# Cross-attention and quantised feed-forward on one core: accumulating copies, half-wise waits of the first key product, and a reordered VectorE queue

## The reference

```
x   = x + attention(layernorm(x), ctx, ctx, mask)     # 16 heads of 64, softmax over 361
out = x + ffn(layernorm(x))                           # 256 -> 1024, gelu, 1024 -> 256
```

## Time and profile before

| | us |
|---|---|
| median of 3 runs | 1116.12 (1115.36 to 1117.17) |
| the profiled execution, its own time | 1116.15 |
| its span, first to last instruction | 1114.3 |
| mean granted TensorE clock | 0.992 |
| PE busy | 1026.3 (92%) |
| DVE busy | 982.0 (88%) |
| ACT busy | 866.6 (78%) |
| POOL busy | 770.5 (69%) |

### The profile page before, as it was taken

How to read it: one execution, slowest core, us unless ns; L and a number is a source line. 1 busy time by engine, 2 the same in 40 slices (tenths; PEclk the granted TensorE clock), 3 DMA queues, 4 the chain that set the end, 5 groups by cost and what they waited for, 6 DMA issues and landing times.

```text
span 1114.3 us, 37739 instructions
## 1 busy us (share of the span) xinstructions
PE 1026.3 (92%) x10639; PEld 649.0 (58%) x10639; DVE 982.0 (88%) x2538; ACT 866.6 (78%) x1809; POOL 770.5 (69%) x1106
## 2 busy tenths in 40 slices
PE   4999999999999999999999999999999999998828
PEld 2555566666666666666666666666666666665317
DVE  5776999999999999999999999999999999996997
ACT  4555888888888888888888888888888888886906
POOL 2337777777777777777777777777777777774800
PEclk9999999999999999999999999999999999999969
DMA  8301665555555555555555555555555555554003
GB/s 260 109 1 29 130 131 136 136 132 132 131 129 135 136 136 136 134 129 133 136 133 129 134 132 129 135 136 129 128 135 136 135 131 129 132 136 143 1 0 119
DMA packets 435437, 136.77 MB, mean 123 GB/s; under 512 B 407666, under 2 KB 434390, under 8 KB 435414
## 3 DMA queue, kind: packets, MB, share of 16 engines
q1 hardware_dynamic: 435414, 136.47, 51.0%
HBM read 28.60 MB, written 6.55 MB: 32 GB/s over the span
## 4 chain that ended last, share of the span: by engine, by line
PE 75%; DVE 10%; ACT 6%; issue 4%; POOL 3%; DVEq 1%; DMA 1%; ACTq 1%; SPq 0%; POOLq 0%
PE front L366 19%; PE front L368 17%; PE front L367 17%; PE back L1300 8%; PE front L1278 6%; PE tp L1278 5%; POOL hl L610 3%; DVE hrange L1129 2%; DVE hrange L1130 2%; DVE prob L979 2%; ACT prob L736 2%; DVE k_l L1028 1%; ACT q_h L790 1%; ACT ctx_h L786 1%; PE front L1415 1%
## 5 line engine op out<-in xcount | busy, mean ns | idle before, releaser
L610 POOL TENSOR_TENSOR hl<-prob,hl 100x361 f16<-100x361 f32 x511 | 432.0, 855 | 96.6 <-DVE hl L986 50.7
L736 ACT ACTIVATE prob<-prob,nmax 100x361 f32<-100x361 f32 x512 | 293.8, 586 | 47.7 <-DVE nmax L979 47.6
L366 PE MATMUL front<-ctx_h,wk_h 128*128 128x362 f16 x512 | 164.2, 321 | 31.6 <-POOL ctx_l L599 18.0
L1300 PEld LDWEIGHTS back<-v,pT 128*128 128x128 f16 (+1 forms) x4608 | 163.9, 97 | 38.9 <-issue 9.6
L742 ACT ACTIVATE hl<-prob 100x361 f16<-100x361 f32 x352 | 176.1, 500 | 7.9
L1300 PE MATMUL back<-v,pT 128*128 128x65 f16 (+1 forms) x4608 | 172.8, 193 | 0.6 <-DMA pT<-hl 0.5
L368 PE MATMUL front<-ctx_h,wk_l 128*128 128x362 f16 x512 | 161.7, 316 | 0.0
L367 PE MATMUL front<-ctx_l,wk_h 128*128 128x362 f16 x512 | 161.5, 315 | 0.0
L746 ACT ACTIVATE k_h<-front 128x362 f16<-128x362 f32 x256 | 119.0, 465 | 54.6 <-PE front L368 54.6
L1028 DVE SCALAR_TENSOR_TENSOR k_l<-front,k_h 128x362 f16<-128x362 f32 x256 | 135.2, 528 | 24.3 <-ACT k_h L746 21.6
L979 DVE CUSTOM_DVE_ANT_0 prob<-front,mask_g,ngain 100x361 f32<-100x361 f32 x256 | 149.6, 585 | 2.3
(11 more groups left out here) (205 smaller groups left out, 2006.5 us busy)
## 6 DMA issues: line engine op xcount, KB each, us to landing
ctx_raw<-ctxT SPq DMA_DIRECT2D x33, 361.0 KB, 3.2
pT<-hl SPq DMA_TRANSPOSE x253, 3.1
xs<-x SPq DMA_DIRECT2D x8, 400.0 KB
q_all<-x SPq DMA_DIRECT2D x32, 100.0 KB
out<-q_all SPq DMA_DIRECT2D x32, 100.0 KB
xb<-out SPq DMA_DIRECT2D x5, 640.0 KB, 8.1
out<-xb SPq DMA_DIRECT2D x25, 128.0 KB, 1.8
q_all<-wq SPq DMA_DIRECT2D x1, 1024.0 KB, 6.3
```

What stands on the lines that cost most here:

```text
L366: eng.matmul(dst, lh, rh, start=first, stop=False)
L610: pool.tensor_tensor(hl[0:T, n % RT, 1, 0:S], prob[0:T, n % RP, 0:S], hl[0:T, n % RT, 0, 0:S], ALU.subtract).then_inc(s_lo, 1)
L736: act.activation(prob[0:T, n % RP, 0:S], prob[0:T, n % RP, 0:S], ACT.Exp, bias=nmax[0:T, n:n + 1], scale=-1.0).then_inc(s_exp, 1)
L1300: ins = pe.matmul(obank[j % 2][:, n % GH * DV:(n % GH + 1) * DV], pT[0:r, n % RT, part_ * ST + st, :], v2[half][0:r, st, v, n % HT, :], st ...
```

## The change

Four edits:

1. HV on DVE is no longer a copy but a `tensor_scalar` (times 1, plus 0) that also accumulates a row sum into a scratch column `hsum`, which nobody reads.
2. TensorE's first key product waits for half k of the context ahead of the three matmuls of half k.
3. LN2 and LN3 write their extremes into a column per item of a new tile `ext`; LN4 is dropped, and one reduction over the columns (LE) is made in the last part. LN2 and LN3 lose their wait on the step before. `LN_STEPS` goes from 5 to 4.
4. In DVE's table MAX14 goes from 9.245 to 10.619 and NORM1 from 10.671 to 10.759. Sorted, the turn then ends with `LN3, HV3` and begins with `K0, MAX14, K1, NORM1, MAX15`; MAX14 belongs to the turn's own item now, so it leaves the first part and is added to the last one.

```
-LN_STEPS = 5
+LN_STEPS = 4
...
     MAX=(-2.253, -1.786, -0.98, -0.598, 0.248, 0.373, 0.602, 1.062, 3.199, 3.682, 5.123, 7.009, 7.8, 8.323,
-        9.245, 12.252),
+        10.619, 12.252),
     HV=(0.09, 2.298, 5.028, 8.693, 12.549),
-    NORM=(8.207, 10.671, 15.577, 16.593),
+    NORM=(8.207, 10.759, 15.577, 16.593),
...
-    LN=(21.545, 22.167, 23.79, 24.463, 24.711))
+    LN=(21.545, 22.167, 23.79, 24.463))
...
-    ("NORM", 1), ("MAX", 15), ("HV", 4), ("PC", 10), ("DL", 14), ("PC", 12), ("PC", 14), ("PC", 15),
+    ("MAX", 14), ("NORM", 1), ("MAX", 15), ("HV", 4), ("PC", 10), ("DL", 14), ("PC", 12), ("PC", 14), ("PC", 15),
...
-    ("LX", 0), ("LX", 1), ("LM", 0), ("LM", 1)]
+    ("LX", 0), ("LX", 1), ("LE", 0), ("LM", 0), ("LM", 1)]
...
+    hsum = place("hsum", [P, 1], F32)
+    ext = place("ext", [P, B, 2], F32)
...
+    def ext_slot(a):
+        return ext[0:T, a:a + 1, :].rearrange("p b w -> p (b w)") if isinstance(a, int) else ext[0:T, a, :]
...
-                    dve.tensor_copy(hl[0:T, h % RT, 0, 0:S], prob[0:T, h % RP, 0:S]).then_inc(s_hv, 1)
+                    dve.tensor_scalar(hl[0:T, h % RT, 0, 0:S], prob[0:T, h % RP, 0:S], 1.0, 0.0, ALU.mult, ALU.add,
+                                      accum_out=hsum[0:T, 0:1]).then_inc(s_hv, 1)
...
+                elif kind == "LE":
+                    dve.tensor_reduce(red[0:T, 0, :], ext[0:T, 0:B - 1, :].rearrange("p b w -> p w b"), AX.X,
+                                      ALU.max).then_inc(s_le, 1)
                 elif kind == "LM":
+                    dve.wait_ge(s_le, 1)
...
-            else:
+            elif n == 1:
                 wait_alone(dve, s_ln, LN_STEPS * a + n)
...
             elif n == 2:
                 wait(dve, s_yn, a + 1)
-                ins = dve.tensor_reduce(row[0:T, 10:11], yn_slot(a), AX.X, ALU.max)
-            elif n == 3:
-                ins = dve.tensor_reduce(row[0:T, 11:12], yn_slot(a), AX.X, ALU.min, negate=True)
+                ins = dve.tensor_reduce(ext_slot(a)[:, 0:1], yn_slot(a), AX.X, ALU.max)
             else:
-                ins = dve.tensor_tensor(red[0:T, 0, :], red[0:T, 0, :], row[0:T, 10:12], ALU.max)
+                ins = dve.tensor_reduce(ext_slot(a)[:, 1:2], yn_slot(a), AX.X, ALU.min, negate=True)
...
-    wait(dve, s_ln, LN_STEPS * B + 1)
+    wait(dve, s_ln, LN_STEPS * B + 2)
...
-                    if n == 0:
-                        wait(pe, s_c, KD * (a + 1))
                     ms = slice(n * P, (n + 1) * P)
                     for k in range(KD):
+                        if n == 0:
+                            wait(pe, s_c, KD * a + k + 1)
```

More of the change, by code:

```diff
@@ L352, in build @@
     s_w16, s_wq = sem("s_w16"), sem("s_wq")
-    s_ln, s_rl, s_yn, s_xb = sem("s_ln"), sem("s_rl"), sem("s_yn"), sem("s_xb")
+    s_ln, s_le, s_rl, s_yn, s_xb = sem("s_ln"), sem("s_le"), sem("s_rl"), sem("s_yn"), sem("s_xb")
     s_rd, s_ar, s_dve = sem("s_rd"), sem("s_ar"), sem("s_dve")
```

## The result

The changed kernel took 1098.99 us (median of 4 runs, 1097.80 to 1099.71) against 1115.84 us beside it: a ratio of 0.9844, with a 95% interval from 0.9832 to 0.9856. 1098.5 us was forecast. Its profiled execution took 1099.71 us, with a span of 1097.6 us.

What follows compares the result with a forecast made beforehand. It took DVE's chain to K3's `k_l`, ahead of V1, as the bound after the change: 0.57 us per item, times 31 is 17.7 us, off 1116.15 us gives 1098.5 us. Range 1091.5 to 1113 us.

Steps and rivals of the forecast that it cites:

- The bound: Between V5 and the next item's V1, DVE is late; TensorE waits 0.58 us for `ctx_l` and 0.41 for `k_l` per item.
- Part 1: Five accumulating HV copies, not held by POOL: 0.52 us each; HV3 occupies 0.45 instead of 1.72 us, HV4 0.45 instead of 0.59.
- HV0's cover: DVE idles 0.32 us after HV0, awaiting the CRED transpose, so its longer copy costs nothing; without that, 0.11 us.
- Part 2: First key product waits per context half: K0 0.47 us earlier, some 0.1 us idle left; `k_h` gains at most 0.19 (0.27 overlapped).
- Part 3: DVE order K0, MAX14, K1, NORM1: no added work; K0's `k_l` starts at 522.20 (522.12 with overlap) against 523.05.
- Part 4: Extremes in columns, LN4 dropped: 0.06 us less per item ahead of MAX14, under cover; taken as 0.
- The sum: K0's `k_l` at 522.16 plus 4.76 us to K3's; V1 at 527.50, 0.57 us earlier per item, 17.7 us in all.
- winning both waits whole: Rival: all of TensorE's `ctx_l` and `k_l` waits won back, 0.99 us per item, 30.7 us: 1085.4 us; 9 in 100.
- nothing to measure: Rival: another engine, such as ScalarE, is late just behind V1 and takes back the gain: 1116 us; 5 in 100.
- The held copy: Rival: POOL holds the accumulating copy like the cast; 0.12 us per item, 1112.4 us; 16 in 100 with cases between.
- The long copy (slower): Rival: accumulating HV4 takes 1.2 us in the chain ahead of V1; 0.18 us lost per item, 1121.7 us; 10 in 100.

Runs made afterwards that it cites:

- a_plain_ts: The changed kernel with HV's `tensor_scalar` without its accumulator: 1115.69 us, ratio 0.9989 to the kernel before.
- b_acc_ext: The kernel before with only the accumulating HV copies and the extremes in columns (LN4 dropped, LE added): 1096.87 us, ratio 0.9823.
- a_fullwait: The changed kernel with TensorE's first key product waiting for both context halves again: 1108.19 us, ratio 0.9921 to the kernel before.
- a_max14_ahead: The changed kernel with MAX14 back at the end of the turn, NORM1 left behind K1: 1095.17 us, ratio 0.9809 to the kernel before.
- a_ln4: The changed kernel with LN4 back behind HV3 in every item, the extremes in columns undone: 1104.53 us, ratio 0.9891 to the kernel before.
- a_oldorder: The changed kernel with DVE's order as before (MAX14 at the turn's end, then K0, NORM1, K1): 1094.85 us, ratio 0.9805 to the kernel before.
- b_acc: The kernel before with the accumulating HV copies alone: 1109.88 us, ratio 0.9936.

## Why the prediction was right

**The bound.** TensorE's two waits and DVE as the late engine between V5 and V1: right. Two loads of the same size on DVE, one inside the chain and one outside, cost 14.8 and 3.8 us, so it is the chain and not the load.

**Part 1.** The duration, 0.52 us drawn on a line between two reductions, was measured as 0.525 (160 copies, 521 to 534 ns), and from start to start 0.44 to 0.45. That nothing holds the copy is shown by its spread beside that of a_plain_ts. One small figure is off: the 0.11 us that HV0 was to cost without its cover takes a duration (0.34) from a time from start to start (0.45); like from like it is 0.18. HV0's cover held: the next DVE instruction starts 0.66 us after it in both kernels.

**Part 2.** K0 was to be done 0.47 us earlier, with some 0.1 us of idleness between its halves, and its `k_h` limited by ScalarE's AH0. K1 followed at 514.62, in the time of before 521.16 against 521.59, so 0.43 earlier; the idleness was 0.14 us in the same count; `k_h` started at 515.06, 521.60 in the time of before, against 521.87. Undone it cost 9.2 us (8.4 expected); alone it gave nothing.

**Part 3.** The sum charged it with +0.52 us for MAX14 in the chain and credited `k_l` ahead of it. The total came out, but the text called the part free of added work and didn't ask what the change would be without it: it would be 4 us faster with part 2 and, by b_acc_ext beside a_fullwait (1096.87 and 1108.19), 11 us faster without part 2. Ahead of K0, MAX14 runs for the most part in the time in which DVE waits for `k_h`: in a_max14_ahead it delays K0's `k_l` by 0.20 us, and not by its 0.52.

**Part 4.** This step was mis-sized. It was taken as 0, at most 0.06 us per item saved. In company with part 1 it is worth 5.5 us with all parts there, and 13.0 us (1109.88 to 1096.87) in the order of before and without part 2. The 0.06 us of the earlier trace rows were LN4's price behind a held cast; the cover was the cast's own wait, and part 1 takes it away. The prediction asked for this of HV0 and LE but not of LN4. That this did no harm to the total is luck: part 4 was in the change. By the prediction's terms the change without it would have had the same forecast, 1098.5 us, and a_ln4 took 1104.53.

**The sum.** K0's `k_l` was forecast at 522.16 and came at 522.09, V1 at 527.50 and came at 527.48; 0.57 us per item were forecast, 0.60 measured. The 17.9 us of 30 intervals, less a start that was 1.3 us later in the profiled execution, give its span but for 0.1 us. That the median came within 0.5 us of the forecast is partly luck: the medians of the kernel before alone differ by 0.8 us. Of the rivals, winning both waits whole is excluded by the 9.6 us ahead of V1, and nothing to measure by the result. The held copy was excluded by the changed kernel's own trace, and its price (1112.4) missed by some 3 us in the two kernels in which it is real (1115.04 and 1115.69). The long copy (slower) is excluded by the 525 ns; its working was right in kind, since 0.45 us more on HV4 took back 14.8 of the 16.9 us.

Open: a_oldorder, a_max14_ahead and b_acc_ext are too close to be ranked (0.9805, 0.9809 and 0.9823, with overlapping intervals). The first two beat the change; the interval of b_acc_ext still touches its own. Part 4 without part 1 was not run.

## What to carry to other kernels

When an instruction's duration spreads widely, look what another engine does under its longest case; if it is held, changing its form can free it, but the next instruction that POOL holds up too can inherit the hold, however small it is. Price each part of a change with its neighbours changed too: here one part was worth 9 us or nothing and another 13 or 5.5, by what else was in the kernel. And follow a chain past the first wait that it ends in (V1), to the second (V2, WO0), before moving work out of it.

## What the runs showed of the hardware

- A one-input SBUF-to-SBUF copy of 100x361 from f32 to f16 on DVE takes 0.34 us when POOL is idle and up to 1.86 when it isn't, as cast or as `tensor_scalar`; the accumulating `tensor_scalar` takes 0.525 us under the same POOL instructions.
- A held instruction can miss the place between two POOL instructions that follow each other without a gap: the cast at 520.75 us lasted through the end of one and all of the next, and so did LN4 in b_acc, of two elements per partition, for 1 us. It need not miss every one: LN4 ended at 521.19 although a third POOL instruction had begun at 521.13. What decides isn't shown.
- The accumulator's read is a second instruction of 83 ns that the next one overlaps: start to start stays 0.07 to 0.08 us below the duration of the copy itself.
- MAX14, waiting for POOL's LO10, started 0.28 us after that one's end in a_max14_ahead, and as long after it in b_acc_ext (514.07 to 514.35). From DVE's `k_l` to TensorE it is 0.05 us, and from POOL's `ctx_l` to TensorE 0.06, so it isn't POOL's signal that is slow as such. It is one pair, at the last step of the loop's turn; the reason isn't shown.
